# A decoder layer's long convolution computed from 16-bit halves, with scales found on the chip and the sums written as additions

## The reference, cut to what matters

```python
x = x + attn(layernorm(x))                       # 32 heads, 8 key groups, rope, alibi, tanh cap
x = x + mixer(ctx, ctx, layernorm(x), ssm_kernel, D)
x = x + ffn(layernorm(x))

# the mixer, for each batch b and head h of 32 (8 channels i, j in a head, 512 positions l):
kv[b, i, j, h, :] = k[b, h, i, :] * v[b, h, j, :]          # here k = v = ctx
y   = causal_convolution(kv, ssm_kernel[h]) + kv * D[h]    # over l
out[b, h, j, :] = sum_i y[b, i, j, h, :] * q[b, h, i, :]
```

## Time and profile before

| quantity | value |
|---|---|
| device time, median of 3 runs | 1182.34 us (1182.04 to 1183.82) |
| span of the profiled execution | 1182.6 us |
| PE busy | 1146.9 us, 97% |
| DVE busy | 877.6 us, 74% |
| POOL busy | 688.9 us, 58% |
| ACT busy | 554.0 us, 47% |
| mean granted clock of PE | 0.995 of full speed |

### The profile page before, as it was taken

The page is one execution under the profiler, slowest core; times in us unless marked ns, Lnnn a source line. Parts: engine busy times, 40 slices in busy tenths (PEclk is TensorE's granted clock), DMA queues, the critical chain, the costliest instruction groups (busy, mean ns, idle before and its releaser), DMA issues. The chain is left out here.

```text
span 1182.6 us, 24878 instructions
## 1 busy us (share of the span) xinstructions
PE 1146.9 (97%) x9715; PEld 794.2 (67%) x9730; DVE 877.6 (74%) x1287; ACT 554.0 (47%) x617; POOL 688.9 (58%) x557
## 2 busy tenths in 40 slices
PE   4888999999999999999999999999999999999998
PEld 4655556657657566566565677777886776786683
DVE  6879878787888787878887688889745745654654
ACT  6766565564755656647556400000244543542441
POOL 1454395784865957849659589999342422423331
PEclk9999999999999999999999999999999999999999
DMA  9563443554445335543455367772012022012000
GB/s 324 156 201 116 121 131 111 164 188 117 125 146 173 122 123 167 187 120 120 129 174 186 116 124 148 143 150 67 1 20 48 7 55 54 18 35 54 19 19 36
DMA packets 166142, 133.48 MB, mean 113 GB/s; under 512 B 69628, under 2 KB 127362, under 8 KB 166082
## 3 DMA queue, kind: packets, MB, share of 16 engines
q1 hardware_dynamic: 141128, 126.44, 36.3%
q10 hardware_dynamic: 24960, 6.29, 3.6%
HBM read 81.76 MB, written 35.21 MB: 99 GB/s over the span
## 5 line engine op out<-in xcount | busy, mean ns | idle before, releaser
L700 PE MATMUL bank<-hT_halves,w_hi 128*128 128x256 f16 x640 | 176.2, 275 | 5.4 <-DVE hT_halves L1419 3.6
L1973 POOL TENSOR_TENSOR parts<-parts 128x512 f32<-128x512 f32 x80 | 118.8, 1489 | 106.8 <-DVE parts L1435 106.8
L701 PE MATMUL bank<-hT_halves,w_hi 128*128 128x256 f16 x640 | 175.8, 275 | 0.0
L702 PE MATMUL bank<-hT_halves,w_lo 128*128 128x256 f16 x640 | 175.8, 275 | 0.0
L952 PE MATMUL bank<-kv,toep 128*128 128x288 f32 (+2 forms) x660 | 159.5, 404 | 0.7 <-ACT qT L1200 0.5
L1978 POOL TENSOR_SCALAR_AFFINE_SELECT region_c<-region_c 128x512 f32<-128x512 f32 x128 | 113.2, 908 | 63.5 <-ACT region_c L1166 63.3
L952 PEld LDWEIGHTS bank<-kv,toep 128*128 128x128 f32 x660 | 124.7, 192 | 34.4 <-ACT qT L1200 0.8
L2121 POOL TENSOR_TENSOR sqsum<-sqsum,toep 128x512 f32<-128x512 f32 x56 | 78.0, 1393 | 95.5 <-ACT toep L1342 95.3
L1991 POOL TENSOR_TENSOR ctx_lo<-ctx,ctx_hi 128x512 f16<-128x512 f32 x64 | 99.0, 1547 | 59.1 <-ACT ctx_hi L1142 59.1
L1163 ACT ACTIVATE region_c<-bank,cap_scale 128x1536 f32<-128x1536 f32 x64 | 98.7, 1542 | 74.2 <-PE bank L768 73.6
L1031 PE MATMUL bank<-odd_halves,guT 128*128 128x256 f16 x512 | 112.2, 273 | 0.0
(11 more groups left out here) (192 smaller groups left out, 2666.4 us busy)
## 6 DMA issues: line engine op xcount, KB each, us to landing
unit_halves<-halves SPq DMA_DIRECT2D x80, 256.0 KB, 2.2
q_both<-unit_halves SPq DMA_DIRECT2D x64, 256.0 KB, 2.9
q_high<-unit_halves SPq DMA_DIRECT2D x64, 128.0 KB, 3.0
toep<-kernel_padded SPq DMA_DIRECT2D x32, 256.0 KB, 3.9
wffn<-w_gu SPq DMA_DIRECT2D x6, 1280.0 KB, 6.2
cpair<-ctx_pairs SPq DMA_DIRECT2D x32, 176.0 KB, 4.8
xin<-x SPq DMA_DIRECT2D x8, 512.0 KB, 3.9
region_o<-wq SPq DMA_DIRECT2D x4, 1024.0 KB, 11.3
```

The source lines that it names most:

```text
L700: pe.matmul(dst, lh, rh, start=first and k == 0, stop=False)
L701: pe.matmul(dst, lh, rl, start=False, stop=False)
L702: mm = pe.matmul(dst, ll, rh, start=False, stop=last and k == n - 1)
L1973: pool.tensor_tensor(slot[:, 0], slot[:, 0], slot[:, 1], ALU.add).then_inc(unit_summed, 1)
```

## The change

**The matmuls take 16-bit halves.** The products `kv` and the Toeplitz kernel are scaled by powers of two and split into two float16 numbers each, high and low. ACT makes the high half of `kv` (`high_kv`, a copy with a scale, 1152 elements a partition), DVE the low half (`low_kv`: kv times the scale minus the high half, 1152 elements, both inputs in SBUF). PE multiplies high by high, low by high and high by low: 30 float16 matmuls a head where there were 10 in float32. ACT also makes 8 of the 36 products, the squares (`square_kv`), so POOL's `products` makes 24 columns in place of 32, and 4 as before.

**The sum of four terms.** The reduction `gather` is replaced, in heads 0 to 28, by `add_terms`: an addition of 512 elements a partition and then, behind a semaphore, one of 256.

**The scales are found on the chip.** ACT squares and sums the whole context, one batch's worth in each pass of the attention (`square_ctx`), through the buffer `xin`, which SP loads once more for it; x of the next batch but one is then loaded behind the placing of units. In the last batch DVE takes the maximum over the batches (`add_skip`), SP writes 128 x 2 numbers to memory and reads them back to all partitions, DVE works out the scales in eight small instructions (`find_conv_scales`), and the kernel is split (`high_kernel` on ACT, `low_kernel` on DVE) and stored. The context and the Toeplitz rows of the first heads are loaded behind that. The undoing of the scale is folded into the residual additions (`scalar_tensor_tensor` for `tensor_tensor`).

**Transfers.** The 12 transposing transfers move from ACT's queue to SP's, between the loads of heads.

```diff
@@ PE, the convolution of a head
-                        d = l - m
-                        mm = pe.matmul(dst, toep[:, n, d * P:(d + 1) * P], kv[:, p, m * B + batches.start:m * B + batches.stop, :],
-                                       start=(m == 0), stop=(m == l))
+                        block = slice((l - m) * P, (l - m + 1) * P)
+                        hi, lo = [kvh[:, p, v, m * B + batches.start:m * B + batches.stop, :] for v in range(2)]
+                        pe.matmul(dst, toep[:, n, 0, block], hi, start=(m == 0), stop=False)
+                        pe.matmul(dst, toep[:, n, 0, block], lo, start=False, stop=False)
+                        mm = pe.matmul(dst, toep[:, n, 1, block], hi, start=False, stop=(m == l))
...
+            def convolve(h, n, q=0):
+                pe.wait_ge(toep_in[n], 16 * (q + 1))
+                pe.wait_ge(kv_lo_done, h + 1)
                 convolve_some(n, slice(0, B), range(LB)).then_inc(y_filled, 1)
@@ ACT
+            def square_ctx(c):
+                act.wait_ge(ctx_in, 16 * (c + 1))
+                act.activation(xin[:], xin[:], ACT.Square, accum_out=ctx_squares[:, bass.ds(c, 1)]).then_inc(ctx_squared, 1)
...
+            def square_kv(h, n, q=0, behind=False):
+                act.wait_ge(cpair_in[n], 16 * (q + 1))
+                if behind:
+                    act.wait_ge(kv_lo_done, h - 1)
+                act.activation(kv[:, n % 2, :, 0:HD], cpair[:, n, :, 0:HD], ACT.Square).then_inc(kv_squared, 1)
+            def high_kv(h, p, behind=False):
+                act.wait_ge(kv_ready, h + 1)
+                act.wait_ge(kv_squared, h + 1)
+                if behind:
+                    act.wait_ge(y_filled, h - 1)
+                act.activation(kvh[:, p, 0], kv[:, p], ACT.Copy, scale=kv_scale).then_inc(kv_hi_done, 1)
@@ DVE
+            def find_conv_scales():
+                dve.wait_ge(scales_moved, 32)
+                dve.tensor_reduce(c_top, tops_all.rearrange("p (q v) -> p v q", v=2), AX_X, ALU.max).then_inc(scale_step, 1)
...
+            def low_kv(h, p):
+                dve.wait_ge(kv_hi_done, h + 1)
+                dve.scalar_tensor_tensor(kvh[:, p, 1], kv[:, p], kv_scale, kvh[:, p, 0], ALU.mult, ALU.subtract
+                                         ).then_inc(kv_lo_done, 1)
...
+            def add_terms(h, p):
+                dve.wait_ge(halved, h + 1)
+                slots, half = prod[:, p], ND * HD // 2
+                dve.tensor_tensor(slots[:, :, 0:half], slots[:, :, 0:half], slots[:, :, half:2 * half], ALU.add).then_inc(terms_added, 1)
+                dve.wait_ge(terms_added, h + 1)
+                out = outT[:, :, :, bass.ds(h, 1), :].rearrange("p l b a r -> p (l b) (a r)")
+                dve.tensor_tensor(out, slots[:, :, 0:HD], slots[:, :, HD:2 * HD], ALU.add).then_inc(mix_done, 1)
...
-            with dve.Fori(1, HM // 2 - 1) as hp:
+            with dve.Fori(1, HM // 2 - 2) as hp:
                 for p in range(2):
                     mix(2 * hp + p, p)
-                    gather(2 * hp + p - 1, 1 - p).then_inc(mix_done, 1)
+                    low_kv(2 * hp + p + 2, p)
+                    add_terms(2 * hp + p - 1, 1 - p)
@@ DVE, last batch of the attention
+                    if step == 4:
+                        add_skip()
+                    if step == 7:
+                        find_conv_scales()
+                    if step == NG + 1:
+                        low_kernel()
...
+                low_kv(0, 0)
                 for i in range(TT):
                     output(b, i, x2r[:, X2_EARLY + i, :])
+                low_kv(1, 1)
@@ POOL
-            with pool.Fori(1, HM // AHEAD) as q:
+            def prepare_kv(h, n, q=0):
+                pool.wait_ge(cpair_in[n], 16 * (q + 1))
+                pool.wait_ge(kv_lo_done, h - 1)
+                products(n)
...
+            with pool.Fori(1, HM // AHEAD - 1) as q:
                 for n in range(AHEAD):
-                    pool.wait_ge(toep_in[n], 32 * (q + 1))
-                    pool.wait_ge(y_filled, AHEAD * q + n - 1)
-                    products(n)
-                    halve(AHEAD * q + n - 2, n % 2)
+                    prepare_kv(AHEAD * q + n, n, q)
+                    halve(AHEAD * q + n - 3, (n + 1) % 2)
@@ SP, ahead of the convolution
+            sp.dma_start(tops_d, tops).then_inc(scales_moved, 16)
+            sp.wait_ge(scales_moved, 16)
+            sp.dma_start(tops_all, tops_d.rearrange("q v -> (q v)").partition_broadcast(P)).then_inc(scales_moved, 16)
...
+            sp.wait_ge(kernel_step, KERNEL_LO)
+            sp.dma_start(kpad_d[:, :, P:P + D], kern_halves).then_inc(scales_moved, 16)
+            for h in range(2):
+                load_pairs(h, h)
```

More of the change, by code:

```diff
@@ L358, in decoder_layer @@
         toep_in = [sem(f"toep_in{p}") for p in range(AHEAD)]
+        cpair_in = [sem(f"cpair_in{p}") for p in range(AHEAD)]
         kv_ready = sem("kv_ready")
+        kv_squared = sem("kv_squared")
+        kv_hi_done = sem("kv_hi_done")
+        kv_lo_done = sem("kv_lo_done")
+        terms_added = sem("terms_added")
         y_filled = sem("y_filled")
@@ L645, in _ @@
                 load_x2(n)
-            for h in range(AHEAD):
[L647 to L652, removed]
+            store_ffn(SHARES - 1)
+            sp.wait_ge(scale_step, 1)
+            sp.wait_ge(kernel_step, KERNEL_SQUARED)
+            sp.dma_start(tops_d, tops).then_inc(scales_moved, 16)
@@ new lines, in _, with turn_weights @@
+            sp.wait_ge(scales_moved, 64)
+            for h in range(2, AHEAD):
+                load_pairs(h, h)
+            for h in range(AHEAD):
+                load_toep(h, h)
+            for h in range(AHEAD, AHEAD + 2):
+                sp.wait_ge(kv_ready, h - AHEAD + 1)
+                sp.wait_ge(kv_squared, h - AHEAD + 1)
+                load_pairs(h, h - AHEAD)
+            def turn_weights(n):
+                if n:
+                    sp.wait_ge(tern_in, 16 * n)
+                if n < GU_TURNS:
+                    rows = slice(n * TURN, (n + 1) * TURN)
+                    sp.dma_start_transpose(guT[:, :, rows], guq_d[rows]).then_inc(tern_in, 16)
+                else:
+                    cols = slice((n - GU_TURNS) * TURN, (n - GU_TURNS + 1) * TURN)
+                    sp.dma_start_transpose(pT[:, cols.start // P:cols.stop // P, :], pq_d[:, cols]).then_inc(tern_in, 16)
@@ new lines, in follow @@
+            def follow(n, h, last=False):
+                sp.wait_ge(y_filled, h + 1)
+                load_toep(h + AHEAD, n)
+                if not last:
+                    sp.wait_ge(kv_ready, h + 3)
+                    sp.wait_ge(kv_squared, h + 3)
+                    load_pairs(h + AHEAD + 2, (n + 2) % AHEAD)
+            sp.wait_ge(quant_stored, QUANT_STORES * (SHARES - 1) + FIRST_QUANT_STORES)
+            for h in range(HM - AHEAD):
+                follow(h % AHEAD, h, h >= HM - AHEAD - 2)
+                if h % 2 == 0 and h // 2 < TURNS:
+                    turn_weights(h // 2)
@@ L1299, in _, with prepare_kv @@
             last_batch()
[L1302 to L1311, removed]
-                    act.dma_start_transpose(pT[:, cols.start // P:cols.stop // P, :], pq_d[:, cols]).then_inc(tern_in, 16)
+            square_kv(2, 2, behind=True)
+            def prepare_kv(h, n, q, last=False):
+                high_kv(h, n % 2, True)
+                if not last:
+                    square_kv(h + 1, (n + 1) % AHEAD, q + (n + 1) // AHEAD, True)
+            for n in range(2, AHEAD):
+                prepare_kv(n, n, 0)
+            with act.Fori(1, HM // AHEAD - 1) as q:
+                for n in range(AHEAD):
+                    prepare_kv(AHEAD * q + n, n, q)
+            for n in range(AHEAD):
+                prepare_kv(HM - AHEAD + n, n, HM // AHEAD - 1, n == AHEAD - 1)
             def stage_out(b):
```

170 lines of the change are left out of this document (129 added, 41 removed).

## The result

| | before | after |
|---|---|---|
| device time, median of 4 runs each | 1183.08 us | 1298.76 us (1297.47 to 1302.56) |
| ratio | | 1.0984, 95% interval 1.0964 to 1.1004 |
| span of the profiled execution | 1182.6 us | 1295.7 us |
| its own time | | 1297.47 us |
| mean granted clock of PE | 0.995 | 0.962 |

What follows compares the result with a forecast made beforehand. PE was taken to bound the mixer, with DVE and POOL close behind. From 1182.6 us, start +10, loop +89 and tail -1 gave 1280.6, less 0.3 for the median: 1280 us, range 1235 to 1300.

Steps and rivals of the forecast that it cites:

- the likeliest case: Mixer loop: DVE and POOL exclude each other and alternate, period 7.7 to 8.5 us, total 1262 to 1294; chance 0.68.
- rival 4: Mixer loop: POOL's `halve` gets in before `low_kv`, 8.74 us a head, total 1297; chance 0.07.
- The loop: Mixer heads 2 to 30: period from 4.85 to 8.14 us by DVE and POOL taking turns; +89 us.
- rival 5: PE's clock in the mixer falls: 7.3 us a head, hidden, some 2 us at the feed-forward net's start; no chance given.
- the half microsecond to "DVE or POOL": Mixer: PE can be relieved by about half a microsecond a head at most before DVE or POOL is the bound.
- The start: Before head 2: delays from the scales' round trip and the first `low_kv`; +10 us, bounds 3 to 18.
- The round trip: Start, scales out and back: stores guessed over at 654.7, DVE 3.4 us late, 2 of it passed to PE.
- The attention: Attention: one ACT square a batch, extra SP transfers and later x loads are hidden; 0 to +3 us, taken as 0.
- The tail: End of the mixer: the last head's float16 matmuls are shorter; -1 us.
- 1 (DVE takes the port twice): Mixer loop: DVE goes again before POOL, or POOL's work is packed; 6.9 or 6.0 us a head, 1246 or 1220; chance 0.15.
- 2 and 3 (no exclusion): Mixer loop: DVE's own 4.74 us a head, 1184, chance 0.06; or PE's relief arrives in full, 1171, chance 0.04.

Runs made afterwards that it cites:

- e3: Changed kernel with POOL's halve adding only 8 numbers and zero-filling the rest, a fill that reads nothing from SBUF; output not the reference's: 1211.66 us.
- e2: Kernel before with only the reduction replaced by the two additions: 1193.81 us, ratio 1.0095 to before.
- e4: Changed kernel with DVE's add_terms ahead of low_kv in the loop, same instructions: 1265.93 us, ratio 1.07.
- e5: Changed kernel with each partition using its own maxima, so DVE does not wait for the round trip; output not the reference's: 1291.01 us.
- e6: Changed kernel squaring seven of eight context pieces, without the load and square at the last batch's first step: 1296.61 us.
- e7: Changed kernel with the scales' maxima written out and read back ahead of the x2 loads on SP: 1295.06 us.
- e1: Changed kernel with the old one-operand reduction in place of the two additions: 1229.82 us, ratio 1.0393 to before.
- e9: Changed kernel with the changes of e1 and e7, and the two low_kv of the start moved behind outputs and statistics: 1223.09 us, ratio 1.0336.

## Why the prediction was right

The forecast was 1280, the measured time 1298.8, inside the range 1235 to 1300, and slower, as 0.91 had it. The direction and the loop are no luck, since the mechanism and its durations came as written. That the range held is in part luck: two terms of the start were too small in the same direction, and 1.2 us were left. The time lies 4.8 us above the likeliest case's own upper end, 1294, and nearer to rival 4's 1297 than to 1280; it is the trace, not the total, that tells the two apart.

- **The loop, +89 forecast, +88.8 measured.** Period 8.14 forecast; 8.10 between the two heads at 796.59 and 804.69; the last two heads 6.9 each (6.6 forecast). The marks named in advance: first addition 2.8 (2.76), second 1.6 (1.47), `low_kv` 1.4 (1.45), `halve` 3.5 (3.42), L2216 1.9 (1.91). What was shown of the mechanism: that the additions are slow only beside a POOL instruction that reads SBUF (e3, by one change), that they cost even with nothing else changed (e2), that the order sets the price (e4). PE's idle time is 3.0 us a head (91.8 over 31) and not 4, since part of its work ran at the lower clock (rival 5's case; it was hidden in the loop, as said, and the 2 us for the net's start did not come). One reading was off without touching the sum: the half microsecond to "DVE or POOL" is DVE's alone (0.51); POOL's idle time in the earlier trace rows is 3.9 us over 28 heads, 0.14 each. The change takes 256 elements a head from POOL, by the prediction's 1.607 ns some 0.4 us, and so moves that bound away.
- **The start, +10 forecast within 3 to 18, +24.6 measured; here the prediction was mis-sized, in two terms.** The first matmul came at 691.91, not near 678, and head 2 at 715.58, not 701.2. The round trip: I let DVE be 3.4 us late, of which 2 were to reach PE, on a guess for the landing, 654.7, that no row carried; it landed at 668.7 and cost 10.1, of which e5 gives back 8.1. The rows of before did show DVE at 652.88 ready to go; what I did not read was how full the queue ahead of those 1 KB was. The attention: "one ACT square a batch, hidden, 0 to +3" stands within its bounds up to the last batch (-0.8 us in this pair of profiles; over all of them the nine kernels with the squares reach the last batch's first scores at 610.4 us on the mean, the two without at 608.6) and failed in the last, where the transfer of `xin` is issued behind the placing of the last units and ACT stands 6.3 us in front of it with the next scores behind: +8.0, of which 5.9 are gone from the trace in e6. The other parts were near: from group 7 to head 0 +5.0 (forecast 3.8 beyond the delay), heads 0 to 2 +3.9 (4.4). Of the 18.8 us between forecast and median, 14.4 are these of the start, and some 3 are that the profiled execution has a span of 1295.7 against the median of 1298.8.
- **The tail, -1: -0.4.**
- **The rivals.** 1 (DVE takes the port twice): did not happen; in every head of the loop for which POOL still had products it got in between the two additions. 2 and 3 (no exclusion) fall with e2 and e3. 4 (`halve` first): `low_kv` of the loop went in ahead of `halve` in every head.

## What to carry to other kernels

Before a vector operation is exchanged for one with less work, count its SBUF operands and see what POOL does at that time: here a reduction with one operand ran beside POOL in its usual 1.93 us, while an addition with two waited for the whole POOL instruction in front of it (2.76 us for 0.7 of work), and the wait looks like work of DVE in the profile: a mean duration above that of the same size elsewhere. Relieving the engine that bounds is worth no more than the distance to the next one, here 0.14 us a head to POOL and 0.51 to DVE, and the work that pays for it must not land on that next one. A small transfer whose result is awaited should not stand on a queue behind megabytes (8.1 us for 1 KB, 3.4 in e7), but moving it ahead only pays what the delayed megabytes leave (3.7 us of the time, where not waiting at all gave 7.8).

## What the runs showed of the hardware that was not expected

- A POOL addition of 8 numbers took 1.31 us, held by a DVE instruction, and 0.20 where DVE had none in (e3), while a POOL fill of 992 elements ran beside a DVE addition untouched, 0.92 us.
- A DVE instruction with only one large SBUF operand, beside two numbers a row, seems to be held too. The two `standardise_x2` at 698.97 in the changed kernel took 2.32 us together, while POOL made products from 698.91 on; before, the two at 679.39 took 1.00 with POOL idle. No run tests this apart.

```profile
698.91 1.48 POOL L2216 TENSOR_TENSOR kv<-cpair 128x768 f32<-128x768 f32 x1
698.97 2.32 DVE L1771 TENSOR_SCALAR hbuf<-x2r,ln_mv,ln_rstd 128x512 f32<-128x512 f32 x2 [1.27 <-POOL ln_rstd L2155]
```

```profile
679.39 1.00 DVE L1638 TENSOR_SCALAR hbuf<-x2r,ln_mv,ln_rstd 128x512 f32<-128x512 f32 x2 [1.26 <-POOL ln_rstd L1962]
```

- PE's mean granted clock from 720 to 820 us was 0.84 in the changed kernel, where PE waits 3.0 us a head, and 1.00 in e1 and e9, where the period is 5.6 us and PE still waits for DVE.
